# Four graph layers on one core: x also laid out turned, low parts and casts shared out anew at the beginning

## What is computed

```python
H_ = jnp.einsum('nd,hde->hne', H, W)                 # _L0
out = jnp.einsum('nm,hme->hne', adj, H_) + b[:, None, :]
...
x = _layernorm(x + _L0_gnn_ref(x, adj, L0_gnn_W, L0_gnn_b), axis=-1)
x = _layernorm(x + _L1_gnn_ref(x, adj, L1_gnn_W, L1_gnn_a), axis=-1)
x = _layernorm(x + _L2_gnn_ref(x, adj, L2_gnn_W1, L2_gnn_b1, L2_gnn_W2, L2_gnn_b2), axis=-1)
x = _layernorm(x + _L3_gnn_ref(x, adj, L3_gnn_W), axis=-1)
```

## Time and profile before

| what | value |
|---|---|
| median of 3 runs | 691.28 us (691.15 to 691.97) |
| the profiled execution | 692.21 us, span 690.5 us |
| TensorE busy | 676.4 us (98%) |
| DVE, ACT, POOL busy | 523.5, 387.8, 147.0 us |
| first layer's aggregation ends | at 82.78 us |
| granted clock, mean | 0.998 |

### The profile page before, as it was taken

The page is one execution under the profiler, slowest core; times in us unless marked ns, Lnnn a source line. Parts: engine busy times, 40 slices in busy tenths (PEclk is TensorE's granted clock), DMA queues, the critical chain, the costliest instruction groups (busy, mean ns, idle before and its releaser), DMA issues.

```text
span 690.5 us, 15604 instructions
## 1 busy us (share of the span) xinstructions
PE 676.4 (98%) x5890; PEld 562.6 (81%) x5890; DVE 523.5 (76%) x969; ACT 387.8 (56%) x503; POOL 147.0 (21%) x239
## 2 busy tenths in 40 slices
PE   5999999999999999999999999999999999999996
PEld 4888844788888888888888888886677778888886
DVE  4877576997998979989899898999443324874564
ACT  7576047888979889798898988743101000222000
POOL 3965522001000000000000000574021102442222
PEclk9999999999999999999999999999999999999999
DMA  8999320001213021030300303013121111211011
GB/s 329 405 347 290 71 72 7 1 1 43 52 32 61 0 68 23 30 61 14 78 0 30 61 0 62 1 32 70 24 51 27 24 25 16 40 39 33 31 52 41
DMA packets 47293, 45.62 MB, mean 66 GB/s; under 512 B 35920, under 2 KB 42000, under 8 KB 45072
## 3 DMA queue, kind: packets, MB, share of 16 engines
q1 hardware_dynamic: 44672, 37.14, 17.7%
q0 software_dynamic: 2016, 7.34, 5.7%
q10 hardware_dynamic: 560, 0.52, 0.2%
HBM read 27.13 MB, written 2.13 MB: 42 GB/s over the span
## 4 chain that ended last, share of the span: by engine, by line
PE 97%; DVE 1%; DMA 1%; issue 0%; ACT 0%; POOL 0%; SPq 0%; POOLq 0%
PE ps L689 16%; PE ps L691 16%; PE ps L690 16%; PE ps L540 16%; PE ps L541 16%; PE ps L531 9%; PE ps L642 6%; DMA x<-in_x 1%; PE ps L496 0%; PE ps L523 0%; DVE x L753 0%; POOL rstd L1145 0%; DVE adj L721 0%; ACT ring_hl L341 0%; ACT arena L350 0%
## 5 line engine op out<-in xcount | busy, mean ns | idle before, releaser
L691 PE MATMUL ps<-arena,ring_hl 128*128 (+1 forms) x1024 | 279.6, 273 | 0.0
L689 PE MATMUL ps<-arena,ring_hl 128*128 (+1 forms) x1024 | 278.8, 272 | 0.0
L690 PE MATMUL ps<-arena,ring_hl 128*128 (+1 forms) x1024 | 278.6, 272 | 0.0
L540 PE MATMUL ps<-arena,adj 128*128 128x256 f16 (+1 forms) x1008 | 223.2, 273 | 0.5 <-issue 0.5
L541 PE MATMUL ps<-arena,adj 128*128 128x256 f16 x1008 | 223.1, 273 | 0.0
L1013 DVE SCALAR_TENSOR_TENSOR ring_a<-rho,gam,ring_a 128x1024 f32<-128x1024 f32 x128 | 163.9, 1281 | 18.0 <-ACT ring_a L430 18.0
L1018 DVE TENSOR_TENSOR ring_hl<-ring_a,ring_hl 128x1024 f16<-128x1024 f32 x128 | 157.0, 1227 | 6.0 <-ACT ring_hl L444 5.8
L444 ACT ACTIVATE ring_hl<-ring_a 128x1024 f16<-128x1024 f32 x128 | 135.2, 1056 | 43.4 <-PE ps L691 31.0
L430 ACT ACTIVATE ring_a<-adj,shift 128x1024 f32<-128x1024 bf16 x128 | 145.5, 1138 | 0.0
L540 PEld LDWEIGHTS ps<-arena,adj 128*128 128x128 bf16 (+1 forms) x1008 | 98.6, 98 | 16.2 <-issue 0.7
L690 PEld LDWEIGHTS ps<-arena,ring_hl 128*128 128x128 f16 x1024 | 99.1, 97 | 13.8
(11 more groups left out here) (99 smaller groups left out, 556.2 us busy)
## 6 DMA issues: line engine op xcount, KB each, us to landing
arena<-in_adj SPq DMA_DIRECT2D x16, 1024.0 KB, 9.2
x<-y POOLq DMA_DIRECT2D x14, 512.0 KB, 5.6
rho<-s_scratch SPq DMA_DIRECT2D x8, 512.0 KB, 3.7
out_x<-x SPq DMA_DIRECT2D x16, 128.0 KB, 1.7
x<-in_x SPq DMA_DIRECT2D x3, 512.0 KB, 7.4
arena<-in_L_gnn_W SPq DMA_DIRECT2D x1, 1024.0 KB, 17.4
arena<-in_L_gnn_a SPq DMA_DIRECT2D x1, 1024.0 KB, 19.4
rho<-in_L_gnn_W SPq DMA_DIRECT2D x2, 512.0 KB, 10.5
```

The lines of the kernel that those rows point to most:

```text
L540: nc.tensor.matmul(ps[:, bank, 0:width], lhs, pp[:, j, 0:width], start=(j == 0), stop=False)
L689: nc.tensor.matmul(acc, hi, v_hi, start=(jt == 0), stop=False)
L690: nc.tensor.matmul(ps[:, b, 0:D], hi, v_lo, start=False, stop=False)
L691: ins = nc.tensor.matmul(acc, lo, v_hi, start=False, stop=(jt == T - 1))
```

## The change

The host lays x out once more, turned (`x_turned`: feature by tile and node), and SP loads this first, into the place that w1 and a take later. ACT casts it straight into `xt` in nine chunks; DVE makes the low parts of the first six tiles and POOL those of the other ten, in five chunks of two tiles. There are no transposes on TensorE, no `take_t` and no split parts of x by tile. w0 comes in two halves with separate semaphores. TensorE runs 28 matmuls on a zeroed tile first. The projections have four PSUM banks in place of two, and `due` puts nearly all aggregation behind the projections. DVE casts pieces 0 and 2 only, ACT all others: 1, 3, 4, 5 and 6 behind its last `take_p`, then 7 to 15 one by one behind the high parts of normalised tiles, which move from DVE to ACT (`gat_hi`). x itself is loaded in four parts among the adjacency pieces: parts 0 and 1 around piece 4, w1 and a behind piece 5, parts 2 and 3 around piece 8; pieces 14 and 15 come behind the later layers' weights. POOL adds the bias behind its low parts, waiting for each part of x; the products of w1 and a go one behind each tile's low part, which itself runs two tiles behind `inv_std`.

```diff
+    WARM = 28
...
+        bias0 = y[:, BANKS - 1, :]
+        warm = y[:, 0, 0:P // 2].bitcast(F16)
...
+        xts = part(arena, (PSET + STAGES * SW, PSET + STAGES * SW + T * D), F32, "p (t c) -> p t c", t=T)
...
+        CHUNKS = [(0, 1), (1, 2)] + [(t, t + 2) for t in range(2, T, 2)]
+        def xt_loaded(t):
+            return ld_xt[t // R + 1 if t else 0], 16
         def cast_done(n):
-            if n < FIRST_CASTS or n == FIRST_CASTS + 1:
-                return s_cast, (FIRST_LOADS.index(n) if n < STAGES else min(n, FIRST_CASTS)) + 1
-            return s_cast_act, max(n - FIRST_CASTS, 1)
+            if n < STAGES:
+                return (s_cast_act if n % 2 else s_cast), n // 2 + 1
+            return s_cast_act, n + 1 - STAGES // 2
...
-            sp.dma_start(x[:, 0, :], xr[:, 0, :]).then_inc(ld_x[0], 16)
+            sp.dma_start(xts[:, 0, :], xt_in[:, 0, :]).then_inc(ld_xt[0], 16)
             for r in range(R):
                 first = max(r * R, 1)
-                sp.dma_start(x[:, first:(r + 1) * R, :], xr[:, first:(r + 1) * R, :]).then_inc(ld_x[r + 1], 16)
-            sp.dma_start(bias0, b0_in.rearrange("(a n) -> a n", a=1).partition_broadcast(P)).then_inc(ld_b, 16)
+                sp.dma_start(xts[:, first:(r + 1) * R, :], xt_in[:, first:(r + 1) * R, :]).then_inc(ld_xt[r + 1], 16)
             adj_n = adj_in.rearrange("c h p w -> (c h) p w")
             def load_adj(n):
                 sp.dma_start(stage[:, n % STAGES, :], adj_n[n]).then_inc(ld_adj[n % STAGES], 16)
             for n in FIRST_LOADS:
                 load_adj(n)
+            sp.dma_start(bias0, b0_in.rearrange("(a n) -> a n", a=1).partition_broadcast(P)).then_inc(ld_b, 16)
+            def load_x(r):
+                sp.dma_start(x[:, r * R:(r + 1) * R, :], xr[:, r * R:(r + 1) * R, :]).then_inc(ld_x[r], 16)
+            load_x(0)
+            load_adj(4)
+            load_x(1)
+            load_adj(5)
+            sp.wait_ge(s_lo, T)
             sp.dma_start(w1f, w1_in.rearrange("(k p) (h f) -> p k h f", p=P, h=H)).then_inc(ld_w1, 16)
             sp.dma_start(abc.rearrange("p h s f -> p (h s f)"),
                          a_in.rearrange("h f a -> a (h f)").partition_broadcast(P)).then_inc(ld_a, 16)
-            load_adj(STAGES)
-            load_adj(STAGES + 1)
+            load_adj(6)
+            load_adj(7)
+            load_x(2)
+            load_adj(8)
+            load_x(3)
+            for n in range(9, NL - 2):
+                load_adj(n)
             sp.dma_start(part(r_flat, (0, 4 * D), F32, "p (c f) -> p c f", c=4),
                          w2a_in.rearrange("(c p) f -> p c f", p=P)).then_inc(ld_w2a, 16)
             sp.dma_start(part(r_flat, (4 * D, 8 * D), F32, "p (c f) -> p c f", c=4),
                          w2b_in.rearrange("(c p) f -> p c f", p=P)).then_inc(ld_w2b, 16)
             sp.dma_start(w3f, w3_in.rearrange("(k p) f -> p k f", p=P)).then_inc(ld_w3, 16)
-            for n in range(STAGES + 2, NL):
+            for n in range(NL - 2, NL):
...
+            w0r = w0_in.rearrange("(k p) h e -> p k (h e)", p=P)
+            for kk in range(K2):
+                act.dma_start(w0f[:, kk, :], w0r[:, kk, :]).then_inc(ld_w0[kk], 16)
+            def w0_hi(kk):
+                act.wait_ge(ld_w0[kk], 16)
+                nc.scalar.activation(w0[:, 0, kk, :], w0f[:, kk, :], ACT.Copy, scale=WS)\
+                  .then_inc(s_wh if kk == K2 - 1 else s_w0h, 1)
...
+            def turned_hi(lo, hi):
+                act.wait_ge(*xt_loaded(lo))
+                nc.scalar.activation(xt[:, lo:hi, 0:D], xts[:, lo:hi, :], ACT.Copy).then_inc(s_hi, hi - lo)
+            turned_hi(*CHUNKS[0])
+            w0_hi(0)
+            w0_hi(1)
+            for chunk in CHUNKS[1:5]:
+                turned_hi(*chunk)
+            turned_after = {0: 5, 1: 6, 3: 7, 5: 8}
+            for t in range(T):
+                take_p(0, t, t % R)
+                if t in turned_after:
+                    turned_hi(*CHUNKS[turned_after[t]])
...
+            def gat_hi(t):
+                act.wait_ge(s_norm, t + 1)
+                if t >= BANKS:
+                    act.wait_ge(*turned(1, t - BANKS))
+                nc.scalar.activation(xg[:, t % BANKS, 0, :], x[:, t, :], ACT.Copy).then_inc(s_hi, 1)
+            for n in (1, 3, 4, 5):
                 cast_n(n)
+            w1_hi(0)
+            w1_hi(1)
+            cast_n(6)
+            CAST = cast_n
+            behind = {0: [(CAST, 7)], 3: [(CAST, 8)], 4: [(CAST, 9)], 5: [(CAST, 10)], 6: [(CAST, 11)], 7: [(CAST, 12)],
+                      8: [(CAST, 13)], 9: [(CAST, 14)], 10: [(w2_hi,)], 11: [(CAST, 15)], 12: [(was_hi,)], 13: [(w3_hi,)]}
+            for t in range(T):
+                gat_hi(t)
+                for step, *n in behind.get(t, []):
+                    step(*n)
...
+            pe.wait_ge(s_warm, 1)
+            for _ in range(WARM):
+                nc.tensor.matmul(ps[:, 0, 0:P], warm, warm, start=True, stop=True)
             def columns_cast(j):
                 if j == 0:
                     pe.wait_ge(s_one, 1)
                 if j % JH == 0:
                     pe.wait_ge(*cast_done(STAGES // 2 + j // JH))
-            joint(0, 0, lambda t: 2 * (t + 1 - T) + T - 1, columns_cast)
+            joint(0, 0, lambda t: max(2 * (t + 3 - T), 0), columns_cast)
...
-                if k is not None:
+                if k in (3, 4):
                     late_.append(split)
...
+            def turned_lo(lo, hi):
+                dve.wait_ge(s_hi, hi)
+                nc.vector.tensor_sub(xt[:, lo:hi, D:2 * D], xts[:, lo:hi, :], xt[:, lo:hi, 0:D]).then_inc(s_lo, hi - lo)
+            turned_lo(*CHUNKS[0])
+            for kk, hi_made, lo_made in ((0, s_w0h, s_w0l), (1, s_wh, s_wl)):
+                dve.wait_ge(hi_made, 1)
+                nc.vector.scalar_tensor_tensor(w0[:, 1, kk, :], w0f[:, kk, :], WS, w0[:, 0, kk, :],
+                                               op0=ALU.mult, op1=ALU.subtract).then_inc(lo_made, 1)
+            for chunk in CHUNKS[1:4]:
+                turned_lo(*chunk)
+            casts_after = {9: 0, 12: 2}
+            for t in range(T):
+                take(0, t, t % R)
+                if t in casts_after:
+                    cast_n(casts_after[t])
...
+            fill = {t: [lambda t=t: sum_products(t - R)] for t in range(R, R + 4 * K2)}
+            fill[8].append(lambda: weight_lo(1, w1, w1ff, [0]))
+            fill[9].append(lambda: weight_lo(1, w1, w1ff, [1]))
+            fill[13] = [was_lo]
...
+            nc.gpsimd.memset(warm, 0.0).then_inc(s_warm, 1)
...
+            pool.wait_ge(s_lo, CHUNKS[4][0])
+            for lo, hi in CHUNKS[4:]:
+                pool.wait_ge(s_hi, hi)
+                nc.gpsimd.tensor_sub(xt[:, lo:hi, D:2 * D], xts[:, lo:hi, :], xt[:, lo:hi, 0:D]).then_inc(s_lo, hi - lo)
             pool.wait_ge(ld_b, 16)
-            def add_b0(t, u):
-                pool.wait_ge(s_lo, t + 1)
-                nc.gpsimd.tensor_tensor(tile_of(x, t), tile_of(x, t), bias0, ALU.add).then_inc(s_xb, 1)
-            tiles(pool, 0, T, add_b0)
-            pool.wait_ge(ld_w1, 16)
-            pool.wait_ge(ld_a, 16)
...
-            for t in range(T):
-                inv_std(t, t % R)
-                prep_lo(1, t, t % R, x)
+            for t in range(T + 2):
+                if t < T:
+                    inv_std(t, t % R)
+                if t >= 2:
+                    prep_lo(1, t - 2, (t - 2) % R, x)
+                if 0 <= t - 2 < 4 * K2:
+                    product(t - 2)
...
+    host["x_turned"] = host["x"].reshape(n // p, p, -1, p).transpose(3, 0, 2, 1).reshape(p, n // p, -1)
```

More of the change, by code:

```diff
@@ L490, in _ @@
         def _(pe):
-            def transpose(k, t, u):
-                pe.wait_ge(s_lo, t + (k * T + 1))
-                if not (isinstance(t, int) and k == 0 and t < 2):
-                    pe.wait_ge(s_xt, t - 1)
-                for c in range(2 * K2):
-                    ins = nc.tensor.transpose(tbank[u % 2][:, c * P:(c + 1) * P],
-                                              xs[:, u, c // K2, (c % K2) * P:(c % K2 + 1) * P], ident[:, :])
-                ins.then_inc(s_t, 1)
             TERMS = [(0, 0), (0, 1), (1, 0)]
@@ L530, in project @@
                 for n, (a, b, kk) in enumerate(steps):
+                    if k == 0 and isinstance(t, int) and t == 0 and n == len(TERMS):
+                        pe.wait_ge(s_wl, 1)
                     ins = nc.tensor.matmul(bank[:, 0:width], xpart(a, kk), w[:, b, kk, :],
@@ L762, in first @@
                 def first():
-                    if a == 0 and isinstance(t, int) and t == 0:
-                        dve.wait_ge(s_xb, T)
+                    if a == 0:
+                        dve.wait_ge(s_xb, t + 1)
                     dve.wait_ge(s_acc, q + 1)
@@ L1124, in _, with product @@
             pool.wait_ge(s_nh, 3)
+            pool.wait_ge(s_lo, CHUNKS[4][0])
+            for lo, hi in CHUNKS[4:]:
+                pool.wait_ge(s_hi, hi)
```

(15 more changed lines are left out.)

122 lines of the change are left out of this document (33 added, 89 removed).

## The result

The changed kernel took 705.58 us (median of 5, 704.65 to 706.71) against 691.56 for the kernel before beside it (691.15 to 693.08): ratio 1.020, interval 1.0186 to 1.0213. It is slower by 14.0 us, where 5.7 were forecast and 700.0 was the high end. The profiled execution of after took 704.68 us with a span of 702.9.

The account below looks back on a forecast made before the run. TensorE, busy 98% of the span, was taken as the bound. The 7.6 us gained early are lost waiting for x, plus 0.7; later cast waits bring E from 82.78 to 88.5, +5.7: 697.0 us, range 693.0 to 700.0.

Parts of the forecast that it names:

- The joint part: First layer's aggregation, four output tiles done jointly: forecast to end at 32.9 us against 40.5 before, a gain of 7.6.
- S: Moment at which the joint part of the first layer's aggregation ends: forecast 32.9 us, against 40.5 before.
- POOL's five low parts: Low parts of ten tiles of x, 512 columns each: 1.27 us apiece taken, 3.5 the other end, finished near 16.6.
- The four additions: POOL's last four bias additions, waiting for x's fourth piece: 0.75 us each, 3.0 in all.
- cast 8: ACT's cast behind tile 3's high part: forecast to end at B + 9.0, where output tile 8 was due at B + 7.6.
- Rival 3: Faster: best case 689.8 us (-1.5), or 683.7 (-7.6) without the wait for x; decided by cast 7 ending before 49.3; chance 0.05.
- rival 2: Only the first wait, for x, counts and every later cast is in time: 691.9 us (+0.6); chance 0.10.
- x's landing: Fourth piece of x, behind adjacency piece 8 on SP's queue: forecast to land at 43.4 us, floor 41.5.
- the first transposing transfer: SP's transfer behind the last load, holding tile 8's high part and cast 13 on ACT: forecast to land at B + 26.2.
- rival 4: The array falls to its lower clock in the 2.5 us idle before cast 13 too: up to 2.7 us more, 699.7; chance 0.15.
- E: Moment at which the first layer's aggregation ends: forecast to move from 82.78 to 88.5 us, +5.7.
- The absorbed stretch: Half pace after the 8.3 us stall: 2.7 us lost, but casts 8 and 9 come late anyway, so E hardly moves.

Follow-up runs that it names:

- x_early: Changed kernel with all four parts of x issued on SP ahead of adjacency piece 4: 695.82 us, ratio 1.006.
- casts_early: Changed kernel with ACT's casts 13 to 15 moved up behind tile 7, ahead of tile 8's high part: 700.22 us, ratio 1.0124.
- pool_late: Changed kernel with POOL's bias additions of tiles 8 to 15 put behind the inverse deviations of tiles 3 and 4: 694.64 us, ratio 1.0053.
- b12_behind_casts: Changed kernel with ACT's two transfers of later biases issued behind casts 1 and 3 instead of ahead of cast 1: 705.54 us, ratio 1.020.
- a_behind_x3: Changed kernel with the load of a (1.05 MB) behind the fourth part of x instead of ahead of it: 702.17 us, ratio 1.0155.
- after_fill: Changed kernel with 76 dummy matmuls on TensorE ahead of the wait for cast 13: 702.87 us, ratio 1.0171.
- fill_first_stall: Changed kernel with 190 dummy matmuls on TensorE ahead of the wait for cast 7: 704.94 us, ratio 1.0188.
- w1_late: Changed kernel with x_early's and casts_early's edits, adjacency pieces 6 and 7 ahead of w1 and a, w1's high parts behind tile 2: 688.93 us, ratio 0.9969.
- w1_late_products: w1_late with POOL's products of w1 and a one tile later: 689.03 us, ratio 0.9959.

## Why the prediction was right and wrong

**Right, with their numbers.** The joint part ended 7.0 us sooner than before, for a forecast of 7.6 (S is 33.5 by the row that 40.5 was read from, and 32.9 was forecast), and all of it was given back. POOL's five low parts ended at 15.3, for 16.6:

```profile
9.72 5.62 POOL L1147 TENSOR_TENSOR ring_hl<-arena,ring_hl 128x512 f16<-128x512 f32 x5 [6.86 <-DVE ring_hl L939]
```

That is 1.12 each: the bound of 1.27 by the nearest row was the good one and 3.5 far off. The four additions took 2.76 for 3.0, and tile 0's way from there to the end of cast 7 another 3.5 for 3.6. With B for tile 0 normalised, cast 8 ended at B + 9.1 (forecast 9.0) and cast 11 at B + 17.7 (17.5). The order on POOL, SP and ACT was read rightly: x_early, casts_early and pool_late each remove the wait that it names. Rival 3 is out, since cast 7 ended at 52.9 and not before 49.3, and rival 2, since TensorE waited 4.03 us for cast 13.

**The first term that was too small: x's landing, 43.4 for 46.66 (+3.3; B came out +3.0, at 50.7).** The forecast let adjacency piece 5 go out into an empty queue, behind cast 1 at 22.9, so that its data would start at 23.65. That step failed: the queue was not empty. Cast 1 ended at 24.4 (the last `take_p` ended 0.7 late, and the two DMA issues by ACT of 1.17 us in all held the cast by 0.84 more; I had counted the queues of SP and POOL and not ACT's own) and piece 5 was issued at 24.45. SP's queue had been given 8.52 MB ahead of it. What it had moved from 0 to 24.45 and from 0 to 26.64 (packets, MB, share of the engines):

```profile
q1 hardware_dynamic: 2183, 7.98, 88.4%
...
q1 hardware_dynamic: 2561, 8.54, 87.4%
```

So piece 5's data started at 26.6, 3.0 us after the forecast, and the rest took 0.3 longer than forecast. One slow stretch ahead of it is seen below: around 20 us, 309 of 322 packets were under 2 KB and some 200 GB/s moved. Whether cast 1's delay of 1.5 us cost anything is open: the data ahead of piece 5 went on flowing for 2.1 us after its issue. (b12_behind_casts, meant to settle this, moved the cast by 0.16 us only.) DMA throughput of after from 16 to 48 us, in slices of 0.8 us:

```profile
GB/s 420 430 440 342 183 181 348 392 407 443 356 370 324 426 428 415 389 415 384 445 425 425 451 379 451 399 440 430 367 379 378 433 440 343 375 385 424 449 379 451
```

The slices from 24.0 to 44.8 average 402 GB/s where I put 425: 7.35 MB take 18.3 us and not 17.3, of which I had allowed 0.6 for short packets. a_behind_x3 confirms that the bytes in the queue set the landing, and their price: 1.05 MB less, 2.4 us.

**The second: the first transposing transfer, B + 26.2 for B + 28.3 (+2.1).** I forecast piece 13 to leave at B + 12.7 and 11.0 us of bytes behind it. It left at B + 12.3, and the bytes did take 11 us. But the queue had run dry, which this row of DMA throughput (55 to 82 us, slices of 0.675) shows:

```profile
GB/s 449 425 425 36 36 0 0 0 158 85 413 437 401 158 121 437 413 449 300 384 385 363 343 422 425 425 425 388 425 401 377 213 26 46 152 0 62 145 67 127
```

Next to nothing moves from 57 to 61.7, and little again from 63.8 to 65.1. Each piece is issued only when a cast frees its place, and it flows in full only 2 us later: piece 12 was issued at 59.76, a first 0.07 MB moved at about 60.7 and the bulk from 61.75; piece 13 left behind cast 9 at 63.0, and from 65.1 to 76.2 the queue is full. SP's queue of after:

```profile
59.76 3.55 SPq L255 DMA_DIRECT2D arena<-in_adj  x2
...
68.78 33.55 SPq L289 DMA_TRANSPOSE ring_hl<-y  x16
```

A queue fed by one cast at a time shows that latency; a full one hides it. For x I had put 0.75 us for it, here nothing. The sum for cast 13 thus became B + 30.5 in place of 28.5, and TensorE waited 4.03.

**The third: rival 4, chance 0.15, was what happened.** The array fell to its lower level at the wait for cast 13 as well, though only 1.1 us after it had gone on. From 81.33 to E are 14.1 us, where the forecast had 12.3 at full pace: 1.8, and after_fill gained 1.7 of it. I had priced it at up to 2.7. The Trainium skill (TensorE: Matmul & The Clock Gate, section "Part 1: The HAM clock gate") says that an idle array drops and must be busy again before it is fast. The trace agrees, at 0.50 behind both long waits. I had believed it for 8.3 us and doubted it for 2.5, with the 1.56 us of the earlier trace rows as my one counterexample; the wait came out at 4.03, and all six waits of 4.0 to 4.5 us in these runs were followed by the lower level.

**The absorbed stretch was read rightly.** After the first wait TensorE ran at half pace for 5.6 us, and this cost nothing, since casts 8 and 9 were due no sooner. fill_first_stall shows it: with the clock held up, TensorE waits 0.65 and 1.23 there, and the time is 0.6 us less.

**The sum.** 3.0 (x) + 2.0 (first transposing transfer) + 1.8 (clock) = 6.8 us, against a miss of E of 95.44 - 88.5 = 6.9. The 1.4 us from there to the miss of the medians, 14.0 - 5.7 = 8.3, is the scatter of the executions, the profiled ones lying 0.9 below (after) and 0.65 above (before) the medians of their five, less 0.2 behind E. The split is that of one execution: x's landing alone lies between 45.90 and 48.10 in the profiled executions of four other kernels that load the same bytes ahead of it (fill_first_stall, after_fill, b12_behind_casts, casts_early). The range was too narrow because its high end held rival 4 alone. I worked out both-sided bounds for the cost of single operations and took the two landings, each a sum over a queue of 4 to 16 MB, without any; and all three terms push the same way: each late landing makes a wait longer, and the longer waits of these runs were those behind which the clock fell.

**What beats both kernels.** The change's loads and casts in another order: w1_late at 688.93 us and w1_late_products at 689.03 (ratios 0.9969 and 0.9959) are 0.3 to 0.4% faster than before. Of the 7.0 us gained at S about 2.5 reach the end. E of the last two lies 5 us ahead of before's, and the next path, the last tiles' transposing transfers behind E, takes the rest.

## What to carry to other kernels

When an engine's work is reordered by hand, follow each first wait on each queue to the transfer it hangs on. Here one addition of a bias, needed much later, held back the normalisation, a cast and the whole array by 10 us, and moving it (on POOL) or its load (on SP) was enough. Give every landing its own range: how full the queue is when the transfer is issued is worth as much as its bytes. And a wait on the critical engine costs more than its length when the clock falls behind it (1.7 us at cast 13), whereas the same fall costs next to nothing where what follows is late anyway.
